# An attention and mixture-of-experts block on one core: q and the MoE weight loaded first, the first quarters of G and Bf as split products, two long warm-up products in place of seven short ones and four fillers, and two remainders moved from VectorE to GpSimd

## The reference

```python
w_eff = quantize(weight + lora_delta) * scale + lora_delta      # cond: levels of an 8-entry codebook
x = x + attention(x @ w_eff.T; Wqkv, bqkv, Wo, bo)              # one head of 128, softmax over 128 keys
base = x @ W.T                                                   # cond2: dense part of the experts
logits = x @ Wr.T + 5 * onehot(language);  top 2, softmax        # gates of 8 experts
lora_out = sum_e gate_e * (x @ A_e.T) @ B_e.T                    # rank 16 each
x = x + (base + 2 * lora_out) @ (s * (q - zero_point)).T + bias  # ffn: q is an int32 weight
```

## Time and profile before

| what | value |
|---|---|
| median of 3 executions | 108.63 us (107.9 to 108.68) |
| the profiled execution | 108.59 us, of which the span of the profile is 106.6 us |
| PE busy | 102.3 us, 96% of the span |
| DVE, ACT, POOL busy | 68.7, 52.1, 31.7 us (65%, 49%, 30%) |
| DMA | 9.57 MB in all; loads run until about 25 us |

### The profile page before, as it was taken

How to read it: one execution, slowest core, us unless ns; L and a number is a source line. 1 busy time by engine, 2 the same in 40 slices (tenths; PEclk the granted TensorE clock), 3 DMA queues, 4 the chain that set the end, 5 groups by cost and what they waited for, 6 DMA issues and landing times.

```text
span 106.6 us, 1460 instructions
## 1 busy us (share of the span) xinstructions
PE 102.3 (96%) x513; PEld 84.6 (79%) x513; DVE 68.7 (65%) x164; ACT 52.1 (49%) x92; POOL 31.7 (30%) x40
## 2 busy tenths in 40 slices
PE   6999999999999999999999999999999999999980
PEld 6747758889788889899888786888899888888850
DVE  4358799979999999814999853004946802482441
ACT  4038989999989960845122239272028104002000
POOL 4000045799907590199100037400000400000000
PEclk9999999999999999999999999999999999999999
DMA  1798999980000000000000000000000550000072
GB/s 45 204 312 268 412 399 405 406 318 6 0 3 0 0 0 0 3 6 0 0 0 0 0 0 0 6 0 0 0 0 0 208 185 0 6 0 0 3 295 98
DMA packets 4471, 9.57 MB, mean 90 GB/s; under 512 B 752, under 2 KB 1008, under 8 KB 4464
## 3 DMA queue, kind: packets, MB, share of 16 engines
q1 hardware_dynamic: 4384, 9.35, 24.5%
q10 hardware_dynamic: 80, 0.13, 0.4%
HBM read 7.38 MB, written 2.10 MB: 89 GB/s over the span
## 4 chain that ended last, share of the span: by engine, by line
PE 92%; DVE 2%; ACT 1%; DVEq 1%; issue 0%
PE psum L861 19%; PE psum L863 19%; PE psum L862 19%; PE psum L887 7%; PE psum L878 5%; PE psum L869 4%; PE psum L897 3%; PE psum L912 3%; PE psum L903 3%; PE psum L907 3%; PE psum L1012 2%; PE psum L1033 2%; PE psum L1027 2%; ACT moe L462 1%; PE psum L1019 1%; PE psum L928 1%
## 5 line engine op out<-in xcount | busy, mean ns | idle before, releaser
L663 DVE COPY_PREDICATED cond_work<-cond_work,psum 128x1024 f32<-128x1024 int32 x10 | 13.7, 1368 | 1.2 <-ACT cond_work L363 0.8
L861 PE MATMUL psum<-G_hi,xT_hi 128*128 128x512 f32 x32 | 12.7, 398 | 0.0
L863 PE MATMUL psum<-G_hi,xT_lo 128*128 128x512 f32 x32 | 12.5, 390 | 0.0
L862 PE MATMUL psum<-G_lo,xT_hi 128*128 128x512 f32 x32 | 12.5, 390 | 0.0
L363 ACT ACTIVATE cond_work<-cond_n,cut_bias 128x1024 f32<-128x1024 f32 x10 | 11.3, 1145 | 0.6 <-DVE cond_n L700 0.6
L578 POOL TENSOR_TENSOR hl<-hl,hl_bias 128x272 f32<-128x272 f32 (+2 forms) x4 | 3.1, 772 | 26.3 <-ACT hl L374 14.4
L523 POOL TENSOR_TENSOR xT_lo<-xT,xT_hi 128x1024 fp32r<-128x1024 f32 x4 | 9.6, 2405 | 3.2 <-DVE cond_work L669 3.2
L861 PE MATMUL psum<-xT_hi,split_b_hi 128*128 128x512 f32 x24 | 9.7, 402 | 0.0
L863 PE MATMUL psum<-xT_hi,split_b_lo 128*128 128x512 f32 x24 | 9.4, 392 | 0.0
L862 PE MATMUL psum<-xT_lo,split_b_hi 128*128 128x512 f32 x24 | 9.4, 390 | 0.0
L887 PE MATMUL psum<-hlT,xT 128*128 128x136 f32 x64 | 8.3, 280 | 0.0
(11 more groups left out here) (167 smaller groups left out, 240.3 us busy)
## 6 DMA issues: line engine op xcount, KB each, us to landing
out<-cond_work SPq DMA_DIRECT2D x7, 256.0 KB, 2.1
cond_n<-in_cond_w SPq DMA_DIRECT2D x2, 512.0 KB, 6.8
xT<-in_x_t SPq DMA_DIRECT2D x2, 512.0 KB, 7.9
q_i<-in_q_t SPq DMA_DIRECT2D x4, 256.0 KB, 7.5
moe<-in_moe_w SPq DMA_DIRECT2D x4, 256.0 KB, 7.7
xT<-in_x_t SPq DMA_DIRECT2D x1, 1024.0 KB, 12.7
wqkv_n<-in_wqkv SPq DMA_DIRECT2D x1, 768.0 KB, 10.6
hlT<-in_hl_t SPq DMA_DIRECT2D x1, 272.0 KB, 6.0
```

Of the source, the lines that this page charges most:

```text
L663: dve.copy_predicated(half(level, h), beyond[n % len(beyond)].bitcast(I32), psum[EARLY][:, j + 1:j + 2].to_broadcast([P, 2 * C])).then_inc ...
L861: pe.matmul(out_ap, l_hi, r_hi, start=first, stop=False)
L862: pe.matmul(out_ap, l_hi, r_lo, start=False, stop=False)
L863: return pe.matmul(out_ap, l_lo, r_hi, start=False, stop=last)
```

## The change

Five things change. (1) SP issues q and moe slice 0 ahead of `cond_w0`, and `cond_w1` behind slices 2 and 3. (2) Two warm-up products of 128x512 replace seven of 128x128 and the four fillers behind the LoRA products; the zeroed tile `blank` is four times as wide. (3) `G_product(0)` takes the place of `G_first` and stands ahead of `x_hl(0, 4)`; it needs `moe_hi(0)`, `w_hi(0)` (ScalarE, put between the second and the third copy of delta), `w_full(0)`, `w_lo(0)` (VectorE, put ahead of `w_delta_first`) and `moe_rest(0)` (GpSimd). (4) Bf's slice 0 is a split product too, so `expb_hi` and `expb_lo` are 512 wide instead of 384. (5) The remainders of w_eff slices 0 and 1 go from VectorE to GpSimd, between those of wqkv.

The declarations of semaphores and blank lines are left out of the diff.

```diff
@@ -64,8 +64,7 @@
     LANG_BIAS = 5.0
     EXPERT_SCALE = 32.0 / 16.0
     CODEBOOK_FLOOR = 1e-8
-    WARM_UP = 7
-    FILL = 4
+    WARM_UP = 2
     X_LOADS = ("x0", "x0", "x1", "x1", "x2", "x2", "x2", "x2")
     HL_PARTS = ((0, 1), (2, 3), (4,), (5, 6, 7))
     assert SEQ == P and D == P and ER == P and HL == ER + E and HT == 512 and C == 512
@@ -96,7 +95,7 @@
         ident = sb("ident", [P, P])
         ident_r = sb("ident_r", [P, P], F32R)
-        blank = sb("blank", [P, P])
+        blank = sb("blank", [P, C])
         lora = sb("lora", [P, 2, C])
         hlT = sb("hlT", [P, CT, HL])
         xT = sb("xT", [P, PAIRS, CT, PT])
@@ -287,14 +287,14 @@
             load("lora_b", lora[0:RANK, 0, :], lora_in[0:RANK, 0, :])
             load("small", small[:, :], small_in)
+            load_proj_weights(0)
             load("cond_w0", cond_n[:, 0:2, :], cond_w[:, 0:2, :])
             load("hlT", hlT[:, :, :], hl_t)
             load("x0", xT[:, 0, :, :], x_t[0])
-            load_proj_weights(0)
             load_proj_weights(1)
-            load("cond_w1", cond_n[:, 2:4, :], cond_w[:, 2:4, :])
             load_proj_weights(2)
             load_proj_weights(3)
+            load("cond_w1", cond_n[:, 2:4, :], cond_w[:, 2:4, :])
             load("x1", xT[:, 1, :, :], x_t[1])
             load("woT", woT[:, :, :], wo_t)
             load("exp_b", expb[:, :, :], exp_b)
@@ -389,9 +389,11 @@
             delta_out(0)
             delta_out(1)
-            set_level()
+            moe_hi(0)
+            w_hi(0)
             delta_out(2)
             delta_out(3)
+            set_level()
             beyond_cut(0, 0)
             beyond_cut(1, 0)
             moe_hi(1)
@@ -407,7 +409,7 @@
             x_hi(0)
             beyond_cut(5, 0)
             act.wait_ge(loaded["exp_b"], 16)
-            rounded(expb_hi[:, 1:CT, :], expb[:, 1:CT, :], expb_hi_ready)
+            rounded(expb_hi[:, :, :], expb[:, :, :], expb_hi_ready)
             beyond_cut(6, 0)
             for i in range(CT):
                 act.wait_ge(G_done, i + 1)
@@ -537,15 +539,20 @@
                 pool.wait_ge(wqkv_hi_ready, o + 1)
                 rest(wqkv_lo[:, o, :], wqkv_n[:, o, :], wqkv_hi[:, o, :], wqkv_ready)
+            def w_eff_rest(o):
+                pool.wait_ge(w_eff_hi_ready, o + 1)
+                rest(split_a_lo[:, o, :], level[:, o, :], split_a_hi[:, o, :], w_eff_lo_ready)
             def moe_rest(o):
-                pool.wait_ge(moe_hi_ready, o)
+                pool.wait_ge(moe_hi_ready, o + 1)
                 rest(split_a_lo[:, o, :], moe[:, o, :], split_a_hi[:, o, :], moe_lo_ready)
+            moe_rest(0)
             moe_rest(1)
             moe_rest(2)
             pool.wait_ge(picked, 3)
             moe_rest(3)
-            pool.wait_ge(w_lo_ready, 3)
+            pool.wait_ge(w_lo_ready, CT)
             pool.wait_ge(loaded["cond_w1"], 16)
             pool.wait_ge(delta_ready, CT)
             pool.tensor_tensor(cond_n[:, 2:4, :], cond_n[:, 2:4, :], delta[:, 2:4, :], ALU.add).then_inc(wd_late_ready, 1)
@@ -555,16 +562,17 @@
                 [P, GROUPS // 2, P]), ALU.mult).then_inc(norm_late_ready, 1)
             pool.tensor_copy(half(level, 1), levels[:, 0:1].to_broadcast([P, 2 * C])).then_inc(level_late_set, 1)
             pool.wait_ge(expb_hi_ready, 1)
-            rest(expb_lo[:, 1:CT, :], expb[:, 1:CT, :], expb_hi[:, 1:CT, :], expb_lo_ready)
+            rest(expb_lo[:, :, :], expb[:, :, :], expb_hi[:, :, :], expb_lo_ready)
             x_lo(0)
             pool.wait_ge(w_eff_ready, 2)
             x_lo(1)
+            w_eff_rest(0)
             wqkv_rest(0)
-            pool.wait_ge(w_eff_lo_ready, 2)
+            w_eff_rest(1)
             wqkv_rest(1)
             wqkv_rest(2)
             wqkv_rest(3)
-            pool.wait_ge(w_eff_lo_ready, CT)
+            pool.wait_ge(w_eff_late_lo_ready, 2)
             pool.wait_ge(woT_hi_ready, 1)
             rest(woT_lo, woT[:, :, :], woT_hi, woT_lo_ready)
             x_lo(2)
@@ -641,7 +649,7 @@
                    .then_inc(w_ready, 1)
             def w_lo(o):
-                dve.wait_ge(w_hi_ready, o)
+                dve.wait_ge(w_hi_ready, o + 1)
                 dve.tensor_tensor(split_b_lo[:, o, :], w_ffn[:, o, :], split_b_hi[:, o, :], ALU.subtract)\
                    .then_inc(w_lo_ready, 1)
@@ -673,7 +681,7 @@
             def w_eff_lo(o):
                 dve.wait_ge(w_eff_hi_ready, o + 1)
                 dve.tensor_tensor(split_a_lo[:, o, :], level[:, o, :], split_a_hi[:, o, :], ALU.subtract)\
-                   .then_inc(w_eff_lo_ready, 1)
+                   .then_inc(w_eff_late_lo_ready, 1)
             def G_rest(i):
                 dve.wait_ge(G_hi_ready, i + 1)
@@ -694,12 +702,13 @@
             alone(dve.tensor_tensor(cuts[:, 2:3], cuts[:, 2:3], cuts[:, 3:4], ALU.min))
             dve.tensor_scalar(cut_bias[:, :], cuts[:, :], -CUT_GAIN, None, ALU.mult).then_inc(cut_bias_ready, 1)
+            w_full(0)
+            w_lo(0)
             w_delta_first()
             dve.wait_ge(wd_ready, 1)
             dve.wait_ge(inv_scale_ready, 1)
             dve.tensor_tensor(blocks(0), blocks(0), inv_scale[:, 0:GROUPS // 2].unsqueeze(2).to_broadcast(
                 [P, GROUPS // 2, P]), ALU.mult).then_inc(norm_first_ready, 1)
-            w_full(0)
             pick(0, 0)
             w_full(1)
             pick(1, 0)
@@ -724,8 +733,6 @@
                .then_inc(Bf_lo_ready, 1)
             pick(2, 1)
             pick(3, 1)
-            w_eff_lo(0)
-            w_eff_lo(1)
             pick(4, 1)
             pick(5, 1)
             pick(6, 1)
@@ -864,12 +871,8 @@
             pe.wait_ge(blank_ready, 1)
-            def idle_turns(n):
-                for _ in range(n):
-                    pe.matmul(psum[6][:, 0:P], blank[:, :], blank[:, :], start=True, stop=True)
-            idle_turns(WARM_UP)
+            for _ in range(WARM_UP):
+                pe.matmul(psum[6][:, :], blank[:, 0:P], blank[:, :], start=True, stop=True)
             pe.wait_ge(loaded["lora_b"], 16)
             pe.wait_ge(loaded["lora_a"], 16)
@@ -877,7 +880,6 @@
             for o in range(CT):
                 pe.matmul(psum[o][:, :], lora[:, 0, o * P:(o + 1) * P], lora[:, 1, :], start=True, stop=True)\
                   .then_inc(delta_done, 1)
-            idle_turns(FILL)
             def x_hl(part, bank, batches=None, base=0):
                 for t in (batches or HL_PARTS[part]):
@@ -889,24 +891,19 @@
                 if t == HL_PARTS[part][-1]:
                     mm.then_inc(xhl_done, 1)
-            def G_first():
-                pe.wait_ge(w_ready, 1)
-                pe.wait_ge(loaded["moe0"], 16)
+            def G_product(o):
+                pe.wait_ge(moe_hi_ready, o + 1)
+                pe.wait_ge(w_hi_ready, o + 1)
                 for i in range(CT):
-                    pe.wait_ge(delta_ready, i + 1)
-                    pe.matmul(psum[i][:, :], moe[:, 0, i * P:(i + 1) * P], w_ffn[:, 0, :], start=True, stop=False)
-            def G_product(o):
-                pe.wait_ge(moe_hi_ready, o)
-                pe.wait_ge(w_hi_ready, o)
-                for i in range(CT):
+                    if o == 0:
+                        pe.wait_ge(delta_ready, i + 1)
                     pe.matmul(psum[i][:, :], split_a_hi[:, o, i * P:(i + 1) * P], split_b_hi[:, o, :],
-                              start=False, stop=False)
-                pe.wait_ge(w_lo_ready, o)
+                              start=(o == 0), stop=False)
+                pe.wait_ge(w_lo_ready, o + 1)
                 for i in range(CT):
                     pe.matmul(psum[i][:, :], split_a_hi[:, o, i * P:(i + 1) * P], split_b_lo[:, o, :],
                               start=False, stop=False)
-                pe.wait_ge(moe_lo_ready, o)
+                pe.wait_ge(moe_lo_ready, o + 1)
                 for i in range(CT):
                     s = slice(i * P, (i + 1) * P)
                     pe.matmul(psum[i][:, :], split_a_lo[:, o, s], split_b_hi[:, o, :], start=False, stop=False)
@@ -914,9 +911,9 @@
                         pe.matmul(psum[i][:, s], ident_r[:, :], ident_r[:, :], start=False, stop=True)\
                           .then_inc(G_done, 1)
+            G_product(0)
             pe.wait_ge(loaded["hlT"], 16)
             x_hl(0, 4)
-            G_first()
             G_product(1)
             G_product(2)
             pe.wait_ge(ident_r_ready, 1)
@@ -931,11 +928,10 @@
             pe.wait_ge(loaded["exp_b"], 16)
             pe.wait_ge(hl_raw_ready, 1)
-            pe.matmul(psum[4][:, :], expb[:, 0, :], w_ffn[:, 0, :], start=True, stop=False)
             pe.wait_ge(expb_lo_ready, 1)
-            for o in range(1, CT):
+            for o in range(CT):
                 mm = three(psum[4][:, :], expb_hi[:, o, :], expb_lo[:, o, :], split_b_hi[:, o, :],
-                           split_b_lo[:, o, :], False, o == CT - 1)
+                           split_b_lo[:, o, :], o == 0, o == CT - 1)
```

(5 more changed lines are left out.)

## The result

The changed kernel's median is 112.11 us (110.41 to 112.29, 4 executions) against 108.56 (107.9 to 108.68, 4): slower. The ratio is 1.027, 95% interval 1.021 to 1.032; it leaves out two of the four executions, as over 1.5% longer than the fastest, though one that it keeps (112.02) has the same low clock as they, so it is smaller than the 3.3% between the medians. A second set of six executions of the same kernel gave 111.75, ratio 1.0267.

The account below looks back on a forecast made before the run. PE's amount of work was taken as the bound until another engine makes it wait. VectorE's chain starting D = 2.5 late, less 0.49 cover plus small additions, gave +2.15: 108.59 + 2.15 = 110.7 us, range 109.3 to 111.5.

Parts of the forecast that it names:

- the chain that nearly sets the end: VectorE chain from w_delta_first through norm, cut, pick and w_full(1) to Bf_lo; its delay was to start y_x(0) 2.15 us later.
- D: Delay of the start of w_delta_first on VectorE, from 8.35 to 10.87: 2.5 us.
- the meeting: w_lo(0) on VectorE during GpSimd's moe_rest(0): ends 0.55 after GpSimd, at 10.95; without it, D would be 1.9.
- PE's saving becomes waiting: PE's 1.73 us less work turns into idle time of about 2.4 us before the second slice of G.
- PE's clock falls in the gap: Rival, chance 0.06: PE's clock drops while it stands at 14.6 to 17.0, giving about 112.7 us.
- the first rise: Moment when PE's clock steps from 1.2 to 2.4 GHz and passes go from 0.85 to 0.43 us: about 7.1.
- 0.49 of cover: Spare time between the end of Bf_lo (33.03) and the start of y_x(0) (33.52), taken off D.
- delta's second copy at 7.86: Start of the second copy of delta, 0.22 later than 7.64, after the longer warm-up and LoRA passes.
- the moved loads do nothing more: Beyond bringing slice 0 early, the reordered loads cost nothing; cond_w1 is not wanted before about 23.
- the second wait, at `y_x(0)`: A second short PE idle time before y_x(0), released by Bf_lo, then none.

Follow-up runs that it names:

- b2b: Kernel before with only four clearings of a spare tile added on VectorE ahead of w_delta_first, to delay that chain: 110.65 us, ratio 1.024.
- e5: Changed kernel with the remainder of moe slice 0 made by VectorE behind the norm instead of by GpSimd: 109.90 us, ratio 1.016.
- e2: Changed kernel with GpSimd's first remainder, moe_rest(0), waiting until VectorE's w_lo(0) is done: 111.17 us, ratio 1.025.
- g1: Changed kernel's arithmetic reordered: loads, ScalarE's order, w_lo(0) behind the norm, router products between slice 0's hi and remainder products, old warm-up and fillers: 111.0 us, ratio 1.026.
- b3: Kernel before with two warm-up products of 128x512 and no fillers, nothing else: 108.22 us, ratio 1.0004.
- b4: Kernel before with the remainders of w_eff slices 0 and 1 on GpSimd, nothing else: 108.08 us, ratio 0.9985.
- e1: Changed kernel with eight zero products of 128x128 filling PE's gap between the router products and the second slice of G: 111.01 us, ratio 1.026.
- b1: Kernel before with the changed order of loads alone: 109.55 us, ratio 1.010.
- e3: Changed kernel with w_lo(0) behind the norm of the first half instead of ahead of w_delta_first: 112.01 us, ratio 1.036.
- g2: g1 with the remainder of moe slice 0 on VectorE behind w_lo(0): 109.58 us, ratio 1.0135.

## Why the prediction was right in its cause and low in its time

- **Right: which step does it.** `w_lo(0)` ahead of `w_delta_first` delays the chain that nearly sets the end. D was 2.72 where 2.5 was taken; b2b shows that a delay alone makes such a loss. By the ratio the time is 108.59 x 1.0268 = 111.5, just at the upper end of the range; the medians, 112.11 and 111.75, lie above it. The account of the 0.8 to 1.4 us between 110.7 and these follows.
- **Right: the meeting.** The addition of 0.68 to 1.36 was worked out from a single row, and its tail behind GpSimd's end came to the hundredth; against e5 it is worth 0.57 of D. The rule of the Trainium skill, page "SBUF — State Buffer", section "SBUF: two separate sides", would have had the subtraction run wholly behind GpSimd's, to 10.60 + 0.68 = 11.28; it ended at 11.15. So the measured tail is 0.55 and not 0.68; otherwise the trace agrees, and so do e2 and the subtraction in g1.
- **Right: PE's saving becomes waiting.** One gap of 2.1 (2.4 predicted), released by ACT's rounding of q slice 1, and nothing given back later. In the kernel before, the warm-up (b3) and GpSimd's remainders (b4) cost nothing; in the changed kernel the warm-up is part of D, see below.
- **Wrong, and why the medians lie above the range: "PE's clock falls in the gap", 0.06.** It falls in 7 of 10 executions. Their median is the rival's case, 112.2 where 112.7 was worked out, and lies above the range. The slow time was taken as 3 to 6 us, of which no row showed the lower end; in the trace it was 3.4 (17.6 to 21.0). The three in which the clock held have a median of 110.4, within 0.3 of the forecast. That is in part luck: with the D of the trace and the true cover (next point) the same sum gives 108.59 + 2.5 = 111.1, so these three probably began earlier; none of them was traced. I had no row of a gap after the first rise and took that for a reason against a fall; it was a reason for a larger chance.
- **Wrong: 0.49 of cover.** It set the start of `y_x(0)` in the chain of waits (33.52) against the end of `Bf_lo` in the timeline (33.03). The timeline has both, 33.36 and 33.03, and where PE does wait it starts 0.06 behind `Bf_lo` (b2b: 35.29 against 35.23): 0.27. In the profiled execution `Bf_lo` ends 2.78 later than before (35.81 against 33.03), so the late chain gives 2.78 - 0.27 = 2.51 where 2.15 was forecast, and the clock the other 0.96 of the 3.47.
- **Wrong: delta's second copy at 7.86.** It started at 8.12. In the chain the LoRA passes began at 5.23, not 4.80 (the warm-up took 3.78 instead of 3.4), and the pass whose weights were loaded at 6.74 still took 0.75, so the rise came later than I had set it, at about 7.4 instead of 7.1. The moment of the first rise varies between executions, and D with it (1.63 in e1, 2.72 here); a range for D has to hold that. It moves the kernel before too: where the rise came early in a kernel with the old start, in b4, the addition began at 7.70 instead of 8.35. Against that start e1's D would be 2.28 and e5's 1.71.
- **Half right: "the moved loads do nothing more".** So in the changed kernel's trace, but in the kernel before they cost 1.0% by themselves (b1). Of b1's two waits, slice 0 covers the one for x0 in the changed kernel, and the later `cond_w0` would stay: by my estimate, undoing `w_lo(0)` alone would leave a D of 0.55 to 0.9 (the addition began at 8.91 in b1 and at 9.24 in e3, both times released by `cond_w0`), of which 0.27 is free.
- **Absent: the second wait, at `y_x(0)`.** It is there where the clock holds (0.5 in e1), and covered where it falls. PE's busy time rose by 0.8 instead of falling by 1.5, mostly because of the fall (3.4 us at half speed are 1.7 us more); in e5, where the clock held, it is 101.3, 1.0 less than before.

What stays open is what decides whether the clock falls. PE's idle time was 2.1 to 2.2 in the traces of the changed kernel (it fell in 7 of 10), 2.3 in e3 (4 of 4), but 1.9 in b2b (0 of 4), 1.8 in e2 (0 of 4), 1.4 in e5 (0 of 4) and two of 1.2 and 1.0 in g1 (0 of 6). In b1 it fell once in 4; the traced execution, which did not fall, has a gap of 0.84, and that of the fallen one isn't known. The order is nearly that of the length of the gap, and b1 breaks it; no threshold follows from this.

## What to carry to other kernels

When the busiest engine never waits, find the chain on the other engines that has almost caught up with it, measure its cover from one view, and price a change by what it does to that chain; work saved on the busy engine is only worth something if its next operand comes earlier too. A gap opened in a PE that never stood still has two prices, the gap and the slower products behind it, and the second (here about 1 us in one trace with a gap of 2.1) may come in some executions only. In these traces a subtraction of two SBUF tensors on GpSimd was free only while VectorE had nothing of the affected kinds to do on the path.

## What the runs showed of the hardware beyond this

While GpSimd's two-input subtraction runs, not only VectorE's two-input additions are held (`w_lo(0)`: 0.68 to 1.36 in the changed kernel and 1.77 in g1; the norm: 1.23 to 2.19 in e2), but also one-input forms: a scale of int32 columns (0.54 to 1.55 in g1) and a conversion of eight columns (0.16 to 0.62 in g2 and 0.65 in g1, until GpSimd's instruction was over). GpSimd's own instruction becomes longer where VectorE's came first (1.28 to 2.19 in e2). The predicated copy, whose mask lies in PSUM here, is not held: in the changed kernel it takes 1.37 at 21.31, while GpSimd subtracts from 21.24 to 22.55, and 1.33 at 14.76, while GpSimd is idle. In a trace the held instruction shows as a long one, and in the chain as "issue". The fallen clock was not back at once when PE had work again: PE ran without a pause from 17.3, and the clock stayed at 1.2 GHz until about 21.0.
